# One more product of 512 columns per group, and two result banks instead of four, in a graph-attention pass

## The reference

```python
def _L1_gnn_ref(x, edge_index, W, att_src, att_dst, bias):     # N = 6250 nodes, 4 heads of 32
    ...
    h = (x @ W).reshape(N, H, C)
    ...
    a_src = jnp.einsum('nhc,hc->nh', h, att_src)
    a_dst = jnp.einsum('nhc,hc->nh', h, att_dst)
    e = jax.nn.leaky_relu(a_src[src] + a_dst[dst], NEG_SLOPE)
    m = jax.ops.segment_max(e, dst, num_segments=N)
    e = jnp.exp(e - m[dst])
    s = jax.ops.segment_sum(e, dst, num_segments=N)
    alpha = e / (s[dst] + 1e-16)
    msg = h[src] * alpha[:, :, None]
    out = jax.ops.segment_sum(msg, dst, num_segments=N).reshape(N, H * C)
    return jnp.tanh(out + bias)

edge_index = jnp.stack([src, dst])
x = _layernorm(x + _L0_gnn_ref(x, ...), axis=-1)     # two GCN layers
x = _layernorm(x + _L1_gnn_ref(x, ...), axis=-1)     # graph attention, above
x = _layernorm(x + _L2_gnn_ref(x, ...), axis=-1)     # attention over edges
x = _layernorm(x + _L3_gnn_ref(x, ...), axis=-1)     # message sum
```

## Time and profile before

| what | us |
|---|---|
| median of 3 runs | 15510.65 (15492.6 to 15525.46) |
| profiled execution | 15500.2 |
| its span, first to last instruction | 15498.4 |
| gat pass, start to end | 1784 (9222 to 11006) |
| max pass | 2125 (7080 to 9205) |
| value pass | 1096 (13430 to 14526) |

### The profile page before, as it was taken

How to read it: one execution, slowest core, us unless ns; L and a number is a source line. 1 busy time by engine, 2 the same in 40 slices (tenths; PEclk the granted TensorE clock), 3 DMA queues, 4 the chain that set the end, 5 groups by cost and what they waited for, 6 DMA issues and landing times. The chain is left out here.

```text
span 15498.4 us, 263663 instructions
## 1 busy us (share of the span) xinstructions
PE 11328.4 (73%) x46351; PEld 7994.1 (52%) x46352; DVE 8762.0 (57%) x33002; ACT 3743.4 (24%) x12262; POOL 6938.9 (45%) x7336
## 2 busy tenths in 40 slices
PE   7988888446666359775777779999567777577587
PEld 5666666236666224432222239999544444466444
DVE  4444444858888810126777766666555555566601
ACT  0122222002222000006888862222111111111100
POOL 0277777047777710005777750000077777444200
PEclk9855555665555579888999985555555555566598
DMA  0000000016676547655444452222155555433164
GB/s 25 1 2 2 2 2 2 0 50 197 199 198 195 146 163 269 221 185 109 108 108 107 108 87 63 63 63 63 41 158 156 156 156 156 106 100 100 47 247 167
DMA packets 1812376, 1676.61 MB, mean 108 GB/s; under 512 B 271444, under 2 KB 1664048, under 8 KB 1773712
## 3 DMA queue, kind: packets, MB, share of 16 engines
q1 hardware_dynamic: 1291008, 1199.97, 25.4%
q0 software_dynamic: 234960, 339.86, 10.0%
q10 hardware_dynamic: 286272, 135.29, 3.0%
HBM read 1160.30 MB, written 514.00 MB: 108 GB/s over the span
## 5 line engine op out<-in xcount | busy, mean ns | idle before, releaser
L1408 POOL DMA_INDIRECT acc<-tab_kv,idx x1664 | 1589.3, 955 | 2578.6 <-POOLq L2121 2058.7
L1408 POOL DMA_INDIRECT room<-tab_h,idx x1664 | 1587.0, 954 | 2104.8 <-POOLq L2121 1575.4
L882 POOL DMA_INDIRECT by_dst<-x,h x1568 | 1704.6, 1087 | 1015.7 <-POOLq L2121 537.7
L1487 PE MATMUL banks<-acc,room 128*128 128x512 f32 x3328 | 1642.5, 617 | 535.1 <-ACT acc L1437 391.8
L1489 PE MATMUL banks<-room 128*128 128x132 f32 (+1 forms) x6656 | 1720.2, 415 | 276.5 <-DVE room L1502 230.0
L1437 ACT ACTIVATE acc<-ident,room 128x128 f32<-128x128 f32 x5824 | 1747.0, 387 | 449.9 <-DMA room<-tab_h,idx 425.3
L882 POOL DMA_INDIRECT by_src<-big,h x1568 | 1517.1, 968 | 606.8 <-issue 449.6
L1502 DVE TENSOR_SCALAR room<-ramp,loc 128x128 f32<-128x128 f32 x6656 | 1751.7, 309 | 24.0 <-issue 22.5
L1489 PEld LDWEIGHTS banks<-room 128*128 128x128 f32 x6656 | 1462.6, 302 | 469.4 <-DVE room L1502 196.2
L1487 PEld LDWEIGHTS banks<-acc,room 128*128 128x128 f32 x3328 | 571.4, 191 | 1605.4 <-issue 1480.7
L1455 PE MATMUL banks<-ident,room 128*128 128x128 f32 x3328 | 1091.0, 430 | 315.0 <-DVE room L1502 311.0
(11 more groups left out here) (423 smaller groups left out, 17334.9 us busy)
## 6 DMA issues: line engine op xcount, KB each, us to landing
big<-cells SPq DMA_DIRECT2D x262, 1568.0 KB, 6.4
cells<-acc SPq DMA_DIRECT2D x1985, 64.0 KB, 1.5
cells<-acc ACTq DMA_DIRECT2D x1984, 64.0 KB
head_rows<-room SPq DMA_DIRECT2D x416, 264.0 KB, 3.2
room<-head_rows SPq DMA_DIRECT2D x416, 264.0 KB, 2.8
acc<-w_rows SPq DMA_DIRECT2D x208, 512.0 KB
value_rows<-acc SPq DMA_DIRECT2D x416, 256.0 KB, 2.8
room<-value_rows SPq DMA_DIRECT2D x416, 256.0 KB, 2.8
```

What stands on the lines that cost most here:

```text
L882: pool.indirect_dma_start(self.target, bass.IndirectOffsetOnAxis(self.slots[:, t:t + 1], axis=0), self.rec[:, t, :], None).then_inc(self.s ...
L1408: pool.indirect_dma_start(far[:, m % BODY, 0:row], None, table, bass.IndirectOffsetOnAxis(k.idx[:, m:m + 1], axis=0)).then_inc(k.gathered[ ...
L1487: last = pe.matmul(k.psum[G * (j % MAX_RING) + t][:, :], oh, rhs, start=True, stop=True)
```

## The change

In the gat pass two things change. The result ring has two banks (0 and 1) instead of four, so `multiply` waits until `added` has counted group minus 1. And PE gets a further step, `idle`, right behind `multiply` for the same group: a product of the bf16 identity with 512 columns of a bf16 table that lies in SBUF anyway, written to bank 2 or 3. Nothing reads it, and nothing waits for it. The other passes keep their code. The diff, whole:

```diff
--- before.py
+++ after.py
@@ -1308,7 +1308,9 @@
     near = {"gat": k.nodev[:, :, :].rearrange("p b c -> p (b c)"),
             "logit": k.h[:, :, :].rearrange("p b c -> p (b c)")}.get(kind)
     blocks = k.block_of[which]
-    agg, tb, vb = k.psum[0:SUM_RING], k.psum[4:6], k.psum[6:8]
+    sum_ring = 2 if kind == "gat" else SUM_RING
+    agg, tb, vb = k.psum[0:sum_ring], k.psum[4:6], k.psum[6:8]
+    idle_rows = k.ramp_pair[:, :, :].rearrange("p c i -> p (c i)").unsqueeze(1).to_broadcast([P, 2, 2 * P])
     diag = k.acc[:, 0:MAX_RING * G * H1 * P].rearrange("p (s t h c) -> p s t h c", s=MAX_RING, t=G, h=H1)
     peaks = k.wk[:, 0:2 * H1].rearrange("p (s h) -> p s h", s=2)
     sums = k.wk[:, 0:G * H1].rearrange("p (t h) -> p t h", h=H1)
@@ -1473,7 +1475,7 @@
                 if kind == "max":
                     wait(pe, reduced, g + 1 - MAX_RING)
                 else:
-                    wait(pe, added, g + 1 - SUM_RING)
+                    wait(pe, added, g + 1 - sum_ring)
                 if kind == "sum":
                     arrived(pe, i, j)
                 else:
@@ -1486,11 +1488,16 @@
                         rhs = diag[:, j % MAX_RING, t, :, :].rearrange("p h c -> p (h c)")
                         last = pe.matmul(k.psum[G * (j % MAX_RING) + t][:, :], oh, rhs, start=True, stop=True)
                     else:
-                        last = pe.matmul(agg[j % SUM_RING][:, 0:width], oh, k.gat[:, ring(j) + t, 0:width],
+                        last = pe.matmul(agg[j % sum_ring][:, 0:width], oh, k.gat[:, ring(j) + t, 0:width],
                                          start=(t == 0), stop=(t == G - 1))
                 last.then_inc(matched, 1)
 
-            turns(pe, {"gat": [(5, multiply), (2, look), (0, turn)],
+            def idle(g, i, j):
+
+                pe.matmul(k.psum[2 + j % 2][:, :].rearrange("p (a c) -> p a c", a=2), k.ident_bf[:, :], idle_rows,
+                          start=True, stop=True)
+
+            turns(pe, {"gat": [(5, multiply), (5, idle), (2, look), (0, turn)],
                        "logit": [(2, look), (0, turn)],
                        "value": [(1, multiply)]}.get(kind, [(0, multiply)]))
 
@@ -1509,7 +1516,7 @@
                 dve.wait_ge(matched, g + 1)
                 wait(dve, added, g)
                 mine = k.acc[:, bass.ds(b * width, width)]
-                dve.tensor_tensor(mine, mine, agg[j % SUM_RING][:, 0:width], ALU.add).then_inc(added, 1)
+                dve.tensor_tensor(mine, mine, agg[j % sum_ring][:, 0:width], ALU.add).then_inc(added, 1)
 
             def diagonal(g, i, j):
```

## The result

The kernel after takes 15574.19 us (median, 15555.94 to 15583.66), the kernel before 15523.04 in the same comparison: ratio 1.0037, 95% interval 1.0027 to 1.0047. That is 57 us slower by the ratio and 51 by the two medians. The prediction was 15585, 75 us over before, and "slower by over 0.2%" at 0.66.

A forecast was written before the change was run, and what follows sets the result against it. DVE's 2.10 us turn was taken to bound the gat pass. Slow turns 105 us less 28 back gave 77, taken as 75: 15500.2 + 75 = 15575, plus 10 to the median, 15585; range 15530 to 15730, down to 15500 with A.

The forecast's parts named there:

- The bound: Gat pass: DVE's turn of 2.10 us hides PE's 2.05 at half clock, so a higher clock is worth nothing.
- The product's price: Gat pass on PE: 0.43 us at half clock, turn 2.48 us, 0.38 over DVE's; 276 such groups cost 105 us.
- What comes back: First group of each of 86 slow pieces saves 0.33 of its 0.38 us: 28 us back in the gat pass.
- part 1: The added product in the gat pass: free at full clock, 105 us lost at half clock less 28 back, 77 us.
- Part 2: Two result banks in the gat pass: half a microsecond to spare at full clock, nothing added to PE's 2.48 at half.
- The ring: Two result banks in the gat pass: cost nothing at full clock, add nothing to PE's own 2.48 us at half.
- A: Rival, no change: the product keeps the clock high nearly everywhere, DVE's 2.10 us hides all; 15500.2, median 15511; chance 0.26.
- C: Rival: the gat pass's clock stays at half despite the product, 316 us lost, 15827; chance 0.12.
- D: Rival: two result banks bind at full clock too, 125 us plus half clock's cost, about 15700; chance 0.09.
- B: Rival, faster: DVE's 0.49 us gap before `add` shrinks with PE's clock, 15470 or less; chance 0.03.
- The rule of the Trainium skill: Clock throttled by default, released by sustained matmul activity; busy PE would be at full clock already, product changes nothing: 0.
- What was to be seen: Gat pass: clock 0.75 to 0.9, `add`s 2.10 us apart at full clock, 2.48 at half, looks wait 50 to 110 us.

## Why the prediction was right, and where it was not

**The bound.** DVE's turn of 2.10 us as the bound, so that a rising clock is worth nothing: right. The pass keeps its 1778 us at clocks of 0.54 (ring alone), 0.85 (product alone) and 1.00 (two products), and falls to 1308 when DVE's read goes.

**The product's price.** 0.43 us at half clock, PE's turn 2.48: right, 0.42 and 2.48 in the trace. The clock's mean of 0.79 lies in the range of 0.75 to 0.9 that was given; 42% of the pass is at half clock where 37% was taken. That 37% was only the middle between two other passes, so its nearness is luck. The argument from them was weak too: "the passes with more columns per group have the higher clock" does not fit the value pass, whose two products of 136 columns are fewer than the gat pass has per group, at the higher clock (0.64 against 0.57).

**What comes back.** This term of the sum was mis-sized. With the measured share, 0.42 x 1840 = 773 us, 312 turns at 2.48 and 0.38 each give 119 us; 50 were lost in that trace. So 69 us came back, not the 28 of part 1, which took 86 pieces at 0.33. The table above says where, by estimate. There are 103 pieces. One of 6.8 us holds 2.75 slow turns and should cost 1.05 us; it costs 0.48, so 0.57 come back. The 34 pieces of 13.7 us, 5.5 turns and 2.09 us, cost 1.23 and get back 0.86: the same 0.57, and some 0.3 because PE's turns stay 2.48 us long through the loop's jump [the piece above], while DVE's turn is 0.32 longer there anyway. The part for the jump was left out of the prediction. One of 3.4 us is covered whole, 0.52. That makes 27 + 10 + 29 = 66 of the 69 us. Part 2 had found half a microsecond to spare; part 1 credited 0.33 of it, to the first slow group alone, and by these costs a slow piece uses it all. Both errors, share and what comes back, lean opposite ways, so that 77 came near 50 to 57 is partly luck.

**The ring.** Part 2 said that it costs nothing at full clock, and that at half clock it "adds nothing to PE's own 2.48". The first is right (ring alone, two products). **The second is the step that failed**: with four banks the same product loses 0 us instead of 40 to 57. The argument looked at whether the wait lengthens PE's slow turn, and it doesn't: that is 2.48 us with either ring. With two banks PE has 0.6 us less lead when the clock falls, and the slow pieces reach 13.7 us instead of 6.8. That the lead explains the pieces of 6.8 us is argued from the timelines; the share of the longer pieces is open. Had the change kept four banks, the same sum would have forecast the same loss, and been wrong. That this kernel came out near is luck in that respect.

**The rivals.** A was wrong for this kernel but right for two products. C and D did not come; B did not. The rule of the Trainium skill weighed in part 1 ("TensorE: Matmul & The Clock Gate", Part 1) fares no better, as far as busy time goes, in the run with the ring alone, where PE is busy 1750 of 1790 us at a clock of 0.54.

**What was to be seen.** `add`s 2.10 apart at full clock: yes. 2.48 in slow pieces: only within long ones, and not evenly (2.19, 2.55, 2.41 and 2.48 above); the median of all slow turns without a jump is 2.41. DVE's wait for the looks at 50 to 110 us: 123.

## What to carry to other kernels

Before paying for a higher clock, look at the engine that sets the turn at both clocks: if its distance doesn't move when the clock does, the clock is worth nothing until that engine is relieved, and then it may be worth much (190 of 470 us here). A ring that costs nothing at a steady pace can still cost when an engine's own pace changes, since its buffers are the lead that the engine then uses up; so price a smaller ring at the slow pace over several turns, not for one. A partial rise of the clock, with work added to get it, can lose where both less and more added work don't.

## What the runs showed of the hardware

- Leaving out DVE's read of the block's number into a register, and the address made from it, shortens the turn by 0.57 us (2.10 to 1.53), and the read may cost DVE more than that, since DVE is not shown to be the bound at 1.53; the engine shows no busy time for it. Moving it ahead of `make_hot` and `lower_scores`, 0.48 and 0.15 us long, hides only 0.1 of it. On POOL the same read fits, with an add of 132 columns in about 0.5 us, into a turn of 1.50 us.
- One unread product of 512 bf16 columns a turn of 2.1 us lifts the granted clock from 0.57 to 0.85 with four banks and from 0.54 to 0.79 or 0.82 with two, two lift it to 1.00. With DVE's read left out, one such product gives 1.00 at 1.53 us a turn, and none gives 0.68.
- With the same instructions on PE the slow pieces were 3.4 to 13.7 us long with two banks and 3.4 to 6.8 with four. What sets their length was not found, and 34 of the 40 us that two banks cost lie in those of 13.7 us.
